# The second feed-forward product in eight matmuls instead of nine

## What is computed

```python
h = h @ w1 + b1                      # 128 -> 2 * 341
a, g = jnp.split(h, 2, axis=-1)
h = a * jax.nn.gelu(g, approximate=False)
x = x + h @ w2 + b2                  # 341 -> 128, the second product
```

## Time and profile before

| | |
|---|---|
| median of 3 runs | 1272.28 us (1272.18 to 1272.44) |
| the profiled execution | 1272.77 us, its span 1271.0 us |
| TensorE matmuls | 1237.2 us busy, 97% |
| ScalarE | 1150.3 us, 91% |
| GpSimd | 1103.1 us, 87% |
| VectorE | 1057.1 us, 83% |
| granted TensorE clock, mean | 0.995 |

### The profile page before, as it was taken

The page is one execution under the profiler, slowest core; times in us unless marked ns, Lnnn a source line. Parts: engine busy times, 40 slices in busy tenths (PEclk is TensorE's granted clock), DMA queues, the critical chain, the costliest instruction groups (busy, mean ns, idle before and its releaser), DMA issues.

```text
span 1271.0 us, 39556 instructions
## 1 busy us (share of the span) xinstructions
PE 1237.2 (97%) x14443; PEld 1007.1 (79%) x14443; DVE 1057.1 (83%) x1937; ACT 1150.3 (91%) x3651; POOL 1103.1 (87%) x780
## 2 busy tenths in 40 slices
PE   8999999999999998999989999999999999999997
PEld 4888888888888887667768888888888888887776
DVE  7888888888888886677778999999999999984777
ACT  5999999999999999787769999999999999998886
POOL 4899999999999998477679999999999999984775
PEclk9999999999999999999989999999999999999999
DMA  5222223322232231020011222222222222111323
GB/s 172 53 65 74 73 74 81 79 73 73 73 82 75 67 79 44 26 63 2 1 30 39 54 63 59 57 56 56 57 56 56 61 59 60 48 43 37 89 79 88
DMA packets 64129, 78.59 MB, mean 62 GB/s; under 512 B 7872, under 2 KB 38144, under 8 KB 63936
## 3 DMA queue, kind: packets, MB, share of 16 engines
q1 hardware_dynamic: 63936, 76.06, 23.2%
HBM read 21.72 MB, written 4.26 MB: 20 GB/s over the span
## 4 chain that ended last, share of the span: by engine, by line
PE 86%; ACT 5%; POOL 4%; DVE 2%; issue 2%; DMA 0%; ACTq 0%; SPq 0%; DVEq 0%; POOLq 0%
PE ps L228 68%; PE ps L278 10%; PE ps L288 4%; PE ps L291 4%; POOL t L1393 2%; ACT P L734 2%; POOL P L1393 1%; DVE t L1075 1%; PE ps L233 0%; ACT sqk L710 0%; PE ps L493 0%; ACT PT L726 0%; DMA norm<-X 0%; POOL hxr L1393 0%; DVE t L1086 0%
## 5 line engine op out<-in xcount | busy, mean ns | idle before, releaser
L734 ACT ACTIVATE P<-ps,nm 128x128 f32<-128x128 f32 x1024 | 344.4, 418 | 0.0
L228 PE MATMUL ps<-wqkv,hT 128*128 128x512 f32 x1152 | 317.1, 412 | 7.2 <-DVE t L1075 5.6
L1393 POOL TENSOR_TENSOR t<-t 128x1024 f32<-128x1024 f32 x128 | 305.9, 2390 | 15.9 <-DVE t L1075 10.2
L1393 POOL TENSOR_TENSOR P<-P,rden 128x512 f32<-128x512 f32 x256 | 290.3, 1144 | 25.3 <-DVE rden L1112 23.2
L1393 POOL TENSOR_TENSOR t<-t,rr 128x1024 f32<-128x1024 f32 x128 | 244.0, 1906 | 23.0 <-ACT rr L719 21.9
L228 PEld LDWEIGHTS ps<-wqkv,hT 128*128 128x128 f32 x1152 | 202.8, 190 | 69.6 <-issue 22.5
L734 ACT ACTIVATION_READ_ACCUMULATOR P<-ps,nm 128x1 f32 x1024 | 235.9, 230 | 0.0
L1086 DVE TENSOR_TENSOR t<-ps,tabl 128x512 f32<-128x512 f32 x256 | 164.2, 683 | 40.6 <-ACT sqk L710 37.8
L1393 POOL TENSOR_TENSOR hxr<-hxf,hxr 128x512 fp32r<-128x512 f32 (+1 forms) x93 | 118.3, 1295 | 76.6 <-ACT hxr L792 76.6
L1105 DVE TENSOR_REDUCE nm<-ps 128x4 f32<-128x512 f32 x256 | 173.7, 680 | 6.2 <-PE ps L228 6.1
L726 ACT ACTIVATE PT<-ps 128x1024 f32<-128x1024 f32 x128 | 129.7, 1014 | 29.4 <-PE ps L278 29.2
(11 more groups left out here) (156 smaller groups left out, 2538.7 us busy)
## 6 DMA issues: line engine op xcount, KB each, us to landing
Vs<-Vn SPq DMA_DIRECT2D x224, 128.0 KB, 2.3
B<-rows SPq DMA_DIRECT2D x32, 256.0 KB, 3.1
side<-in_x SPq DMA_DIRECT2D x17, 256.0 KB, 3.0
A<-X SPq DMA_DIRECT2D x16, 256.0 KB, 2.5
norm<-X SPq DMA_DIRECT2D x32, 128.0 KB, 2.2
norm<-X SPq DMA_DIRECT2D x32, 127.8 KB, 2.3
hsh<-X SPq DMA_DIRECT2D x31, 128.0 KB, 2.3
hsh<-X SPq DMA_DIRECT2D x31, 127.8 KB, 2.3
```

Of the source, the lines that this page charges most:

```text
L228: return e.matmul(o, lhsT, rhs, start=start, stop=stop, skip_group_check=True)
L734: k = act(P[:, g, :], ps[:, 3 + s, (g % 4) * 128:(g % 4 + 1) * 128], ACT.Exp, bias=nm[:, g:g + 1], accum_out=den(s)[:, g % 4:g % 4 + 1])
L1393: return e.tensor_tensor(o, a, b_, op)
```

## The change

For b < 15 the 85 rows of chunk 2 are packed. Rounded part and rest of chunk 2 need 3 x 85 = 255 rows of products, and those fit into one matmul of 128 rows and one of 127. The rest is now written to a tile of its own, `lo2`. SyncE copies the 85 rounded rows to the second operand, then 42 rows of the rest to rows 85 to 126 of the first operand, 42 to the same rows of the second, and the last one to row 127 of the first. The weight is laid out to match: a fourth block is loaded and rounded by an instruction of its own, and its rest is made by two instructions in place of one. The product then takes 3 + 3 + 2 = 8 matmuls. The last sequence of each layer keeps nine. ScalarE and GpSimd take the chunks in the order 0, 2, 1, and ScalarE does all three at the end of iteration b, in layer 1 ahead of `rec_scale(b)` and `end_turn(b-2)`. In layer 0, `sums` moves from behind chunk 0 of `up(2)` to behind chunk 1. SyncE's later loads of layer 0 are spread between the packs.

```diff
+        def order(b):
+            return (0, 2, 1) if b < NB - 1 else (0, 1, 2)
@@ tensor: up @@
-                    if l == 0 and b == 2 and j == 0:
+                    if l == 0 and b == 2 and j == 1:
@@ tensor: down @@
+                if b < NB - 1:
+                    for j in range(2):
+                        e.wait_ge(s_hxhi, 3 * m + 2 * j + 1)
+                        e.wait_ge(s_hxlo, 3 * m + 2 * j + 1)
+                        for p, q in THREE:
+                            mm(ps[:, bank, :], w2r[:, q, j, :], hxr[:, b % 2, p, j, :], j == 0 and p > 0, False)
+                    e.wait_ge(s_ph[b % 2], 16 * ((8 - b % 2) * l + b // 2 + 1))
+                    e.wait_ge(s_pk, 48 * (l * (NB - 1) + b + 1))
+                    mm(ps[:, bank, :], w2r[:, 0, 2, :], hxr[:, b % 2, 0, 2, :], False, False)
+                    mm(ps[:, bank, :], w2r[0:127, 1, 2, :], hxr[0:127, b % 2, 1, 2, :], False, True).then_inc(s_y, 1)
+                    return
@@ scalar: loop over b @@
-                    if l and 0 < b < NB:
-                        split_hx(l, b - 1, 0)
-                        split_hx(l, b - 1, 1)
                     if b < NB:
                         gelu(l, b, 0)
+                    if b < NB:
+                        gelu(l, b, 1)
                     if l == 0 and b == 2:
                         square_mean(l, NB - 1, 7)
-                    if 0 < b < NB:
-                        split_hx(l, b - 1, 2)
-                    if b < NB:
-                        gelu(l, b, 1)
...
                             conv(b + 1)
-                            split_hx(l, b, 0)
-                            split_hx(l, b, 1)
+                            for j in order(b):
+                                split_hx(l, b, j)
...
                     if l and b < NB - 1:
+                        for j in order(b):
+                            split_hx(l, b, j)
                         rec_scale(b)
@@ vector: hidden @@
-                    e.wait_ge(s_hxlo, 3 * (m - 1) + j + 1)
+                    e.wait_ge(s_hxlo, 3 * (m - 1) + order(b - 1).index(j) + 1)
@@ gpsimd: split_hx @@
+                if j == 2 and b < NB - 1:
+                    if l or b:
+                        e.wait_ge(s_pk, 48 * (l * (NB - 1) + b))
+                    tt(lo2[0:n, :], hxf[0:n, j, :], hxr[0:n, b % 2, 0, j, :].bitcast(F32), ALU.subtract).then_inc(s_hxlo, 1)
+                    return
@@ sync @@
+            def pack(l, b):
+                m = l * NB + b
+                e.wait_ge(s_hxhi, 3 * m + 2)
+                first, second = hxr[:, b % 2, 0, 2, :].bitcast(F32), hxr[:, b % 2, 1, 2, :].bitcast(F32)
+                rest = lo2.bitcast(F32)
+                e.dma_start(second[0:85, :], first[0:85, :]).then_inc(s_ph[b % 2], 16)
+                e.wait_ge(s_hxlo, 3 * m + 2)
+                e.dma_start(first[85:127, :], rest[0:42, :]).then_inc(s_pk, 16)
+                e.dma_start(second[85:127, :], rest[42:84, :]).then_inc(s_pk, 16)
+                e.dma_start(first[127:128, :].rearrange("p (s k) -> p s k", s=16), rest[84:85, :].rearrange("p (s k) -> p s k", s=16)).then_inc(s_pk, 16)
```

More of the change, by code:

```diff
@@ L110, in program @@
         gl = [side[:, 0, :], side[:, 1, :], room[:]]
+        lo2 = hT[:, 1, 0, :]
         ti = oT[:, 1, :]
@@ L199, in program @@
         s_out = [sem("s_out0"), sem("s_out1")]
+        s_ph = [sem("s_ph0"), sem("s_ph1")]
         s_qkv, s_vm, s_sim, s_tpq, s_tpk, s_tpp, s_av = (
@@ L905, in scalar @@
                     if i == (3 if l else 7):
-                        e.wait_ge(s_w2, 16 * (l + 1))
+                        e.wait_ge(s_w2, 32 * (l + 1))
                         if l:
                             e.wait_ge(s_y, NB)
-                        act(w2r[:, 0, :, :], w2, ACT.Copy).then_inc(s_w2hi, 1)
+                        act(w2r[:, 0, :, :], w2, ACT.Copy)
+                        act(w2r[:, 1, 2, :], w2x, ACT.Copy).then_inc(s_w2hi, 1)
                     if i == NT + 1:
@@ L1448, in split_hx @@
                 m, n = l * NB + b, CH[j][1]
-                e.wait_ge(s_hxhi, 3 * m + j + 1)
+                e.wait_ge(s_hxhi, 3 * m + order(b).index(j) + 1)
+                if j == 2 and b < NB - 1:
[3 more added lines that the diff above has]
+                    return
                 tt(hxr[0:n, b % 2, 1, j, :], hxf[0:n, j, :], hxr[0:n, b % 2, 0, j, :].bitcast(F32),
@@ L1531, in gpsimd @@
                     if 0 <= b - 1 < (NB - 1 if l else NB):
-                        for j in range(3):
+                        for j in order(b - 1):
                             split_hx(l, b - 1, j)
@@ L1569, in load_w2 @@
             def load_w2(l):
-                e.dma_start(w2, d["w2"][:, l]).then_inc(s_w2, 16)
+                e.dma_start(w2, d["w2"][:, l, 0:3]).then_inc(s_w2, 16)
+                e.dma_start(w2x, d["w2"][:, l, 3]).then_inc(s_w2, 16)
             def shift_rows(o, x, landed):
@@ L1676, in sync @@
                     e.dma_start(wraw1[2], d["wqkv"][:, 1, 1024:1536]).then_inc(s_wq2, 16)
[L1677 to L1685, removed]
+                    for b in range(NB - 1):
+                        pack(l, b)
+                        if b == 2:
+                            keep_roots(l, NB - 1)
+                            spread_roots(l, NB - 1)
+                        if b == 4:
+                            e.wait_ge(s_wlo1, 3)
+                            load_tables(1, qs1)
+                            shift_h(1, 0)
+                        if b == 6:
+                            e.wait_ge(s_hn[0], NB)
+                            load_w1(1)
+                            load_w2(1)
+                    shift_h(1, 1)
                 else:
@@ L1689, in sync @@
                         load_x(b, xe[b], b)
+                    for b in range(3):
+                        pack(l, b)
                     keep_roots(l, NB - 1)
@@ L1701, in sync @@
                             load_x(b + 2, xe[b % 2], b % 2)
+                        if b + 3 < NB - 1:
+                            pack(l, b + 3)
                         if b == NB - 4:
@@ L1775 @@
             w2[:n, l, j, :] = a["w2"][l, o:o + n, :]
+        w2[85:127, l, 2, :] = a["w2"][l, 256:298, :]
+        w2[127, l, 2, :] = a["w2"][l, 340, :]
+        w2[85:127, l, 3, :] = a["w2"][l, 298:340, :]
     qks = np.stack([a["q_scale"], a["k_scale"]], 1)
```

10 lines of the change are left out of this document (6 added, 4 removed).

## The result

The changed kernel takes 1277.41 us (median of 11 runs, 1276.10 to 1285.09) where the kernel before, on the same chip, takes 1272.11 us (11 runs, 1271.05 to 1275.37). The ratio is 1.0049, with a 95% interval of 1.0035 to 1.0063: slower by 5.3 us in the medians, some 6 us by the ratio. The forecast was 1274.4 us, with a range of 1269.5 to 1278.5. The time lies inside the range and 3 us above the forecast.

What follows compares the result with a forecast made beforehand. The prediction took TensorE to bound the kernel before, and a ScalarE-VectorE loop to bound layer 1 after. Layer 0's -3.6 and layer 1's +5.7 sum to +2.1 us, so 1274.4 us, range 1269.5 to 1278.5.

Steps and rivals of the forecast that it cites:

- the loop: Layer 1, steady: hidden(b, 2) leads to hidden(b+1, 2) through ScalarE (2.88) and VectorE (4.14); a turn takes 7.02 us, before 6.69.
- T(2) to T(3): Layer 1, from the end of VectorE's third hidden in iteration 2 to that in iteration 3: 10.5 us, with tail_root between.
- layer 0: Layer 0 in all -3.6 us: 2.8 from twelve steady downs at 0.232 each, 0.8 from iterations 2 and 3.
- iterations 2 and 3: Layer 0: later sums let six matmuls fill a wait (1.33 us), a third rounding takes 0.52 back; gain 0.8 us.
- the opening of layer 1: Layer 1 at b = 0: late first gelu and down(0) mostly made up; T(0) to T(2) +0.1 us.
- The transfers thus cost nothing here: Layer 1, steady: packs are in by T + 5.2, and VectorE's down_add needs down only at T + 7.
- an issue: SyncE: each of a pack's three DMA issues takes about 0.5 us, from 461 ns for a 64-row copy.
- the slack of 1 us: Layer 0: pack data there at 557.7, TensorE at the seventh matmul of down(b) at 558.9 or 0.23 earlier; no wait.
- the end: Layer 1 after the last chunk: TensorE is no longer behind, which shortens the end by some 0.3 us.
- Late packs: Rival: packs land late in layer 0, TensorE waits 0.5 us in 13 iterations at a 3.6 landing; 1280.9 us, chance 0.08.
- The rival in which TensorE stays the bound: TensorE bounds both layers, layer 1 at 6.46 us an iteration with no loop; 1265.5 us, chance 0.10.
- the two in which layer 0 keeps its 7.99: GpSimd or third rounding delays TensorE, or two packed matmuls cost as much as three; 1277.2 us, together 0.05.

Runs made afterwards that it cites:

- scale_first: Changed kernel with rec_scale(b) ahead of the three roundings in layer 1, not behind them: 1276.15 us, ratio 1.0019 to the kernel before.
- order_012: Changed kernel without packing (nine matmuls), with chunks rounded and split in the order 0, 1, 2: 1271.59 us in one run, beside one of before at 1272.11.
- no_pack: Changed kernel with its orders on ScalarE and GpSimd, but nine matmuls and no pack: 1279.54 us, ratio 1.0044 to the kernel before.
- loads_later: Changed kernel with layer 1's two loads of x issued behind pack(1), not ahead of pack(0): 1276.34 us, ratio 1.0024 to the kernel before.
- both_split: Changed kernel with layer 1's x loads behind pack(1), and rec_scale between the rounding of chunk 0 and those of 2 and 1: 1273.70 us, ratio 1.0011.
- packs_first: As both_split, but SyncE issues pack(b+3) of layer 1 ahead of the output and load of its iteration: 1274.45 us, ratio 1.0011.
- layer0_only: The change in layer 0 alone; layer 1 keeps the orders, nine matmuls and transfers of before: 1270.17 us, ratio 0.9973 to the kernel before.
- sums_later: The kernel before with only the sums of layer 0 moved behind chunk 1 of up(2): 1272.22 us in one run.

## Why the prediction was right or wrong

**Right: the loop.** It said 7.02 a turn and 10.5 for T(2) to T(3). The trace has 7.00 and 10.49, and the two halves of the sum hold one by one: 2.88 on ScalarE, 4.12 on VectorE where 4.14 was forecast. The run without the packing shows that the order alone makes it, scale_first that it runs through `rec_scale`, and order_012 that one rounding less shortens it by just that rounding. Layer 1 from T(2) to T(15) thus came to +5.7, against +5.95 forecast.

**Right: layer 0.** It said -3.6, and the trace has -3.3. The 0.23 us of a matmul held (no_pack against the changed kernel: 2.87 us for the removed matmuls). Packs land there 3.3 us after the first of the three issues, where the forecast had 3.2, and no seventh matmul waits.

**Wrong in size: iterations 2 and 3.** It said 1.33 - 0.52 = 0.8. The runs have 0.89 for the moved sums and 0.55 back for the new order with its third rounding (25.72 - 25.17), so 0.34. Why the moved sums bring 0.89 and not 1.33 is open. The changed kernel's 26.06 - 25.26 = 0.80 between the first and the fourth `down` only looks like the forecast: it also holds 0.25 of the third `down`, which the forecast counted among its twelve, and 0.20 of the first, which it let vanish into a wait. Against -3.6 for the layer, the missing 0.46 and the unforeseen 0.20 leave -3.3.

**Wrong: the opening of layer 1.** The failed step is "The transfers thus cost nothing here", and with it "TensorE finishes `down(0)` about half a microsecond late as well, for the first pack lands near 1163.8. Both are mostly made up". I had priced the landing of the first pack at the median of the 64-row copies, 3.2 us after the first of its three issues and 2.2 after the last. It lands 5.7 and 4.0 us after them, with 768 KB issued just before it; without two of those three loads ahead it lands 3.9 and 2.15 after them. The trace of before held the warning: the DMA share is 0.32 in this opening and 0.07 in steady layer 0, and the rows of landings had a worst case of 3.6. I used that case against layer 0, where it didn't apply. The term was +0.1 and measured +4.0 to +5.5. loads_later takes 2.9 to 4.4 of it back, the clock's part included.

**A term that I lacked: the clock.** In both profiled executions of the changed kernel the granted clock fell to its lower level within the stall of the opening, for 6.8 and 3.4 us. Nothing in the forecast priced that. It is not a fixed price of the stall: the run of 1276.10 us had no such stretch, and both_split had one behind a stall of 1.57 us.

**Wrong in size: an issue.** I took 0.5 us for each of the pack's issues, from copies of 64 rows at 461 ns. Durations of the three issuing lines after (min/median/max in ns):

```profile
L1665 SPq DMA_DIRECT2D hxr<-hxr x30: 749/775/845, 521.2 to 1266.6; - x30
L1667 SPq DMA_DIRECT2D hxr<-hT x30: 781/803/851, 523.3 to 1267.9; - x30
L1669 SPq DMA_DIRECT2D hxr<-hT x30: 547/547/570, 525.0 to 1269.6; - x30
```

Copies of 85 and 42 rows take 0.75 to 0.85. The last issue begins 1.6 to 1.7 us after the first, not 1.0. In layer 0 the last transfer then lands sooner after its issue than priced (1.7 us, not 2.2), and the slack of 1 us held the rest. In layer 1 it is part of the path that both_split and packs_first met.

**Too small: the end.** -0.3 was forecast and -1.25 measured. The order of before takes 10.77 to 11.67 us from T(15) to the end in its three traces, so one execution's difference is worth only some of that.

**The sum.** By its stretches in the feed-forward stages, without what lies ahead of them and between the layers, the changed kernel is +6.6 us from before in the first execution (-3.3, +5.5, +1.3, +4.3, -1.25) and +5.0 in the second. The medians have +5.3, the forecast +2.1. The difference is the opening. That the time still lies in the range is owed to the range's width and to two smaller errors the other way (the end by 1, the loop by 0.3): the forecast was right about the loop, and lucky about the opening.

**The rivals.** Late packs were a rival, but I had placed them in layer 0. They cost time in layer 1, where large loads stand in front of the first one. The rival in which TensorE stays the bound is out (7.00, not 6.46), and so are the two in which layer 0 keeps its 7.99 (7.77).

**What stays open.** The stretch between the layers is nearly the same code in both kernels (the fourth weight block and SyncE's last shift of rows, which now waits for the last pack, are new), and was 513.3 to 518.4 us long over the eleven traces. It follows the time at the lower clock in it, 0 to 10.2 us, at about 0.5 us for each. It explains 3.2 to 3.7 us of the distance between the profiled spans. Both traces of the changed kernel have the longest such stretch (10.2), but loads_later, scale_first and both_split, with the same code up to there, have 3.4, 0 and 0. Whether it is chance can't be told from eleven traces. At the same 6.8 us of low clock the stretch is 514.7 in before, 516.2 in layer0_only and 515.0 in packs_first, so a part of 1.5 us or less may be the new code's. T(0) of layer 0 was at 518.0 in before and at 518.4 to 520.3 in the others (518.55 in sums_later, whose code up to there is that of before). The fourth weight block may have a part of up to 0.5 us in this.

## What to carry to other kernels

When an instruction moves ahead of others in a queue that runs in order, follow the data from it through every engine back to itself, and add up the durations: here that sum (7.02, with 6.46 for TensorE alone) foretold the steady pace to 0.02 us. Price a new transfer at each place where it is issued, with what is queued before it there, and the first one of a stage most of all; a median landing is no price for a stretch with large loads in the queue. And when one cause is removed, look for the path it covered: in layer 1 three costs stood behind one another (the loads, the loop, the pack's own chain), and the change paid only in layer 0, where none of them was on the path.

## What the runs showed of the hardware

- A copy's issue on SyncE took 461 ns for 64 rows of 2 KB, 0.75 to 0.85 us for 42 or 85 rows, and 0.55 us for one row in 16 pieces.
- The 85-row copy sends 6 landing events, and the three copies of 42, 42 and 1 rows send 46 together. By "DMA: Bandwidth & Descriptors", section "Why a DMA increments its semaphore by 16 and not by 1", of the Trainium skill these would be 5, 14, 14 and 16 engines, with one event from each engine and, below 16 engines, one more from the issuer. The traces agree with that: 5 + 1 = 6 and 14 + 1 + 14 + 1 + 16 = 46. The 85-row copy lands 4.0 us after its issue in layer 0 and 4.35 in steady layer 1. It was 5.33 behind the three loads (5.11 in the second execution).
- With 768 KB issued from 4.5 to 2.9 us ahead of it, a copy of 2 KB in 16 pieces landed 4.0 us after its issue. In loads_later, with only the first 256 KB of these, 4.5 us ahead of it, it landed 2.15 after, and in layer 0 1.7.
- TensorE's granted clock fell from 2.4 to 1.2 GHz within the stalls of 3.3, 2.9 and 2.6 us of the matmuls (the changed kernel twice, scale_first), for 6.8, 3.4 and 3.4 us. The seven stalls of 1.4 to 2.1 us in the feed-forward stage of layer 1 of four kernels had mixed ends: behind those of 1.57 (both_split) and 1.83 us (packs_first) it fell for 3.4 us, behind those of 1.47, 1.53, 1.74, 1.96 and 2.10 us it did not. So the length of a stall alone doesn't tell.
- Between the layers a stretch of 0, 3.4, 6.8 or 10.2 us at the lower clock came and went from execution to execution, and took some 0.5 us for each us.
